# One-hots that read their row of numbers from a PSUM bank instead of SBUF, in a fused graph, attention and expert kernel

## What is computed

```python
def sage(x, src, dst, Wl, bl, Wr):
    agg = segment_sum(x[src], dst, N_NODES)          # gather the source rows, add them per destination
    cnt = segment_sum(ones, dst, N_NODES)
    return (agg / maximum(cnt, 1.0)[:, None]) @ Wl.T + bl + x @ Wr.T

h   = relu(sage(xn, src, dst, W1l, b1, W1r))          # layer 1
gnn = sage(h, src, dst, W2l, b2, W2r)                 # layer 2
mix = layer_norm(mlp(x1) + x1),  x1 = layer_norm(linear_attention(xn) + xn)
x   = x + gnn + mix
x   = x + prob * (gelu(ln(x) @ W1 + b1) @ Wd[expert] + bd[expert])   # the best of 8 experts for each node
```

## Time and profile before

| | us |
|---|---|
| three executions | 2453.99, 2454.78, 2458.47 |
| median | 2454.78 |
| the profiled execution, its own time | 2453.61 |
| its span in the trace | 2451.8 |
| PE busy | 1925.4 (79%) |
| POOL busy | 1702.3 (69%) |
| DVE busy | 1148.8 (47%) |
| ACT busy | 549.0 (22%) |

### The profile page before, as it was taken

How to read it: one execution, slowest core, us unless ns; L and a number is a source line. 1 busy time by engine, 2 the same in 40 slices (tenths; PEclk the granted TensorE clock), 3 DMA queues, 4 the chain that set the end, 5 groups by cost and what they waited for, 6 DMA issues and landing times.

```text
span 2451.8 us, 45561 instructions
## 1 busy us (share of the span) xinstructions
PE 1925.4 (79%) x9589; PEld 1190.2 (49%) x9590; DVE 1148.8 (47%) x3201; ACT 549.0 (22%) x1242; POOL 1702.3 (69%) x1773
## 2 busy tenths in 40 slices
PE   3799988878688887776899999877665543679998
PEld 2455555544455555543455555444332211368886
DVE  8544443433577777764555545433332221242221
ACT  6444333333222222221222222111100000101110
POOL 6777777777777777757777777777777777164442
PEclk9999999898899999997899999988776665689999
DMA  7444444444444444434454555444443333245551
GB/s 219 132 124 126 124 123 121 122 118 118 132 135 137 133 133 137 132 97 149 146 166 151 164 157 164 147 153 142 138 141 116 114 116 105 89 141 167 168 167 63
DMA packets 155000, 332.67 MB, mean 136 GB/s; under 512 B 34853, under 2 KB 89095, under 8 KB 154917
## 3 DMA queue, kind: packets, MB, share of 16 engines
q0 software_dynamic: 85824, 248.21, 34.6%
q10 hardware_dynamic: 42630, 58.35, 6.9%
q1 hardware_dynamic: 26466, 25.33, 3.4%
HBM read 273.97 MB, written 58.72 MB: 136 GB/s over the span
## 4 chain that ended last, share of the span: by engine, by line
PE 36%; POOL 33%; issue 15%; DVE 7%; DMA 4%; DVEq 2%; POOLq 2%; ACT 1%; ACTq 1%; SPq 0%
POOL big L699 32%; PE bank L538 12%; PE bank L1728 8%; PE bank L1496 6%; PE bank L1716 2%; PE bank L1502 2%; DMA mbuf<-qT_d 1%; PE bank L1526 1%; PE bank L1651 1%; PE bank L1521 1%; DMA big<-hh_d,edges 1%; POOL big L709 1%; POOLq L696 1%; DMA big<-xh_d,edges 1%; POOLq L694 1%
## 5 line engine op out<-in xcount | busy, mean ns | idle before, releaser
L699 POOL DMA_INDIRECT big<-xh_d,edges x782 | 769.8, 984 | 240.5 <-issue 232.4
L699 POOL DMA_INDIRECT big<-hh_d,edges x782 | 752.4, 962 | 261.1 <-issue 227.2
L1496 PE MATMUL bank<-big,S 128*128 x1960 | 589.0, 427 | 245.8 <-SPq L604 218.4
L898 DVE SCALAR_TENSOR_TENSOR S<-edges,tv,iota 128x512 f16<-128x512 f16 x490 | 368.6, 754 | 450.5 <-PE bank L1496 267.6
L1496 PEld LDWEIGHTS bank<-big,S 128*128 128x128 f16 x1960 | 203.7, 104 | 533.6 <-issue 389.8
L1494 PE MATMUL bank<-ones,S 128*128 128x1 f16 x980 | 165.4, 169 | 73.7 <-SPq L604 63.6
L538 PE MATMUL bank<-turned,x1T 128*128 128x512 f32 x392 | 195.6, 622 | 0.0
L720 POOL DMA_INDIRECT out_dram<-big,node_s x56 | 56.8, 1014 | 145.1 <-DVE big L1231 141.2
L1494 PEld LDWEIGHTS bank<-ones,S 128*128 128x128 f16 x980 | 95.5, 97 | 89.5 <-SPq L604 75.7
L1424 ACT ACTIVATE x1T<-bank 128x256 f32<-128x256 f32 x49 | 18.8, 383 | 531.7 <-PE bank L1502 531.7
L1231 DVE SCALAR_TENSOR_TENSOR big<-bank,prob_s,res 128x256 f32<-128x256 f32 x56 | 27.1, 484 | 179.4 <-PE bank L1730 179.4
(11 more groups left out here) (228 smaller groups left out, 2910.4 us busy)
## 6 DMA issues: line engine op xcount, KB each, us to landing
hx_d<-mbuf ACTq DMA_DIRECT2D x49, 512.0 KB
big<-xh_d,edges POOLq DMA_INDIRECT x782
big<-hh_d,edges POOLq DMA_INDIRECT x782
big<-in_fwd_dram SPq DMA_DIRECT2D x8, 1024.0 KB, 6.4
qT_d<-abuf ACTq DMA_DIRECT2D x49, 128.0 KB
hh_d<-HL ACTq DMA_DIRECT2D x49, 128.0 KB
mbuf<-qT_d ACTq DMA_DIRECT2D x49, 128.0 KB, 2.6
hx_d<-res ACTq DMA_DIRECT2D x49, 128.0 KB
```

What stands on the lines that cost most here:

```text
L699: e.indirect_dma_start(G[:, r, n % SC, :], None, table, bass.IndirectOffsetOnAxis(ap=srcx[:, n:n + 1], axis=0)).then_inc(d_g[r], 16)
L898: VI.done(e.scalar_tensor_tensor(S[:, walk.u, :, :], dst[:, bass.ds(c * SC, SC)].unsqueeze(2).to_broadcast([P, SC, P]), tv[:, bass.ds(k, 1 ...
L1496: ins = e.matmul(AGG[:], S[:, walk.u, j, :], G[:, bass.ds(slot, 1), j, :].rearrange("p a c -> p (a c)"), start=False, stop=False, skip_gro ...
```

## The change

`numbers_p` is a quarter of the bank `FO`, which now belongs to DVE alone: DVE writes the numbers 0 to 127 there once, in fp32, and every one-hot reads them from there. `iota16` is gone. Another part of the same bank (`m_p`) takes the place of `m_t` in the attention's steps `tz`, `s`, `n2` and `res` (`m_t` stays for layer 2's normalised rows). To free `FO`, layer 1's product goes to the second half of `B5` (`FU`), beside the queries, and layer 2's product to the second half of `FT` (`FV`), beside the turned mean. As two engines are not to be in one bank at once, PE gets two waits: in layer 1, behind `tr1` of tile t, for the ReLU of tile t-1; in layer 2, ahead of `tr1` of tile t, for `x2` of tile t-1.

```diff
-        iota16 = sb("iota16", [P, P], F16)
...
+        FU, FV = B5[:, C:2 * C], FT[:, C:2 * C]
+
+        numbers_p, m_p = FO[:, 0:P], FO[:, C:2 * C]
...
-            step(e.tensor_copy(iota16[:], ii[:, 0:P]))
             step(e.tensor_copy(iof[:, 0:P + 3], ii[:]))
...
+            step(e.tensor_copy(numbers_p, iof[:, 0:P]))
...
                 VI.done(e.scalar_tensor_tensor(
                     S[:, walk.u, :, :], dst[:, bass.ds(c * SC, SC)].unsqueeze(2).to_broadcast([P, SC, P]),
-                    tv[:, bass.ds(k, 1)], iota16[:].unsqueeze(1).to_broadcast([P, SC, P]),
+                    tv[:, bass.ds(k, 1)], numbers_p.unsqueeze(1).to_broadcast([P, SC, P]),
                     ALU.subtract, ALU.is_equal), "S")
...
                 step("tz", at(lambda: e.tensor_tensor(
-                    m_t.rearrange("p (h q m) -> p h q m", h=CH, m=HD), blocks[:, :, 0:P].rearrange("p h (q m) -> p h q m", m=HD),
+                    m_p.rearrange("p (h q m) -> p h q m", h=CH, m=HD), blocks[:, :, 0:P].rearrange("p h (q m) -> p h q m", m=HD),
...
-                step("s", at(lambda: e.scalar_tensor_tensor(m_s[:], xnS, rstd[:, bass.ds(raw(i), 1)], m_t[:], ALU.mult, ALU.add)))
+                step("s", at(lambda: e.scalar_tensor_tensor(m_s[:], xnS, rstd[:, bass.ds(raw(i), 1)], m_p, ALU.mult, ALU.add)))
...
-                step("n2", mo(lambda: e.scalar_tensor_tensor(m_t[:], m_o, lnt[:, 2:3], lng2, ALU.subtract, ALU.mult)))
+                step("n2", mo(lambda: e.scalar_tensor_tensor(m_p, m_o, lnt[:, 2:3], lng2, ALU.subtract, ALU.mult)))
...
-                step("res", mo(lambda: e.scalar_tensor_tensor(res_tile(i - 2), m_t[:], lnt[:, 7:8], res_tile(i - 2),
+                step("res", mo(lambda: e.scalar_tensor_tensor(res_tile(i - 2), m_p, lnt[:, 7:8], res_tile(i - 2),
                                                               ALU.mult, ALU.add)))
...
-                    VX2.done(e.tensor_tensor(res_tile(t), res_tile(t), FO[:, 0:C], ALU.add), "x2")
+                    VX2.done(e.tensor_tensor(res_tile(t), res_tile(t), FV, ALU.add), "x2")
...
-                    AR1.done(e.activation(hb[:], FO[:, 0:C], ACT.Relu), "relu")
+                    AR1.done(e.activation(hb[:], FU, ACT.Relu), "relu")
...
                     clear(AGG[:])
                     clear(CNT[:, 0:1])
                     PT1.done(transposes(FT, 0, mean), "tr1")
+                    AR1.wait(e, "relu", t, 1)
...
                     clear(AGG[:])
+                    VX2.wait(e, "x2", t, 1)
                     PT2.done(transposes(FT, 0, mean), "tr1")
```

More of the change, by code:

```diff
@@ L1520, in out1 @@
                     for h in range(CH):
-                        e.matmul(FO[:, 0:C], xTs[:, h, :], w1r[:, h, :], start=(h == 0), stop=False)
-                    e.matmul(FO[:, 0:C], ones3[:], gb1, start=False, stop=False)
+                        e.matmul(FU, xTs[:, h, :], w1r[:, h, :], start=(h == 0), stop=False)
+                    e.matmul(FU, ones3[:], gb1, start=False, stop=False)
                     if isinstance(t, int):
@@ L1525, in out1 @@
                     for h in range(CH):
-                        ins = e.matmul(FO[:, 0:C], mT[:, h, :], w1l[:, h, :], start=False, stop=(h == CH - 1))
+                        ins = e.matmul(FU, mT[:, h, :], w1l[:, h, :], start=False, stop=(h == CH - 1))
                     PH1.done(ins, "h")
@@ L1628, in out2 @@
                     AM2.wait(e, "mT", t)
-                    PO2.done(matmuls(e, FO[:, 0:C], [(mT[:, h, :], w2l[:, h, :]) for h in range(CH)]), "o")
+                    PO2.done(matmuls(e, FV, [(mT[:, h, :], w2l[:, h, :]) for h in range(CH)]), "o")
                 def trx(t):
```

## The result

The changed kernel takes 2435.86 us (median of 4; 2432.62 to 2436.64), the kernel before 2456.62 us beside it: ratio 0.991, 95% interval 0.9897 to 0.9924, so 20.8 us less. The profiled execution is the longest of its four, 2436.64 us with a span of 2434.8, against the shortest of before (2453.61): between the two profiles lie 17.0 us. Every ratio in this document is taken over the executions in the faster of a chip's two states alone, and so can differ a little from the quotient of the medians beside it.

A forecast was written before the change was run, and what follows sets the result against it. POOL's gathers, at a beat of about 1.25 us, were taken to set the pace except where PE or DVE steps do. Savings of 12.3 + 6.4 + 0.7 + 5.0 = 24.4 us gave 2430 us, range 2424 to 2438.

The forecast's parts named there:

- the first gather of layer 2 would start 19 us earlier: Sign at the start of layer 2: its first gather comes some 19 us earlier if the forecast holds.
- One-hots stop holding gathers.: All 490 one-hots: they no longer lengthen gathers; in the stretch 75 to 635, 12.3 us saved and kept.
- The term of 19.4 us for layer 1: Layer 1: 12.3 us from 75 to 635, plus stage B's 6.4 from one-hots and 0.7 from step `s`.
- It is kept, with 1.5 us to spare: Stage B: its saving of 6.4 and 0.7 us is kept, POOL's least room of 4.4 us exceeding the 2.9 needed.
- the 4.8 us are lost: Layer 2 up to 1362: the 4.8 us of shorter gathers are lost, as POOL waits longer for PE.
- Layer 2 behind 1362: 5.0 us.: Layer 2 behind 1362: 5.0 us saved and kept, since POOL's room grows again.
- A PSUM operand costs nothing.: DVE steps using the bank: price taken as 0, bounded by 63 ns each; the one-hot stays at 754 ns.
- PE's wait for the ReLU is covered.: Layer 1: PE's new wait costs 0; at stage B's tightest tile the ReLU ends 0.78 us before `tr1`.
- dearer operands: Rival, DVE steps with PSUM operands: 63 ns more each, still faster than before, 2436 us; chance 0.14.
- half rate: Rival, one-hots: numbers stream from PSUM at half rate, 0.53 us more each, slower at 2457 to 2458 us; chance 0.05.
- More is kept: Rival: layer 2's early saving isn't lost, or gathers meet remaining two-input steps less often; 29.2 us saved, 2425 us; chance 0.06.
- Doesn't unlock: Rival: something else in the one-hot holds gathers (index operand, fp16 output, length); 2454 us, up to 2460; chance 0.07.

The follow-up runs named there:

- after_again: The changed kernel as it is, compared a second time with the kernel before: 2435.47 us against 2457.55, ratio 0.9909.
- numbers_in_sbuf_again: The changed kernel with the one-hots reading the numbers from SBUF in fp32, on a faster chip: 2461.31 us against 2460.12 for the kernel before, ratio 1.0002.
- waits_only: The kernel before with only TensorE's two new waits added: 2459.43 us against 2457.66, ratio 1.0005.
- psum_layer2_only_again: The changed kernel with layer 1's one-hots reading from SBUF, layer 2's from the bank, on a faster chip: 2455.56 us, ratio 0.9991 to the kernel before.
- psum_layer1_only_again: The changed kernel with layer 2's one-hots reading from SBUF, layer 1's from the bank, on a faster chip: 2440.57 us, ratio 0.9923 to the kernel before.
- numbers_in_sbuf: The changed kernel with the one-hots reading the numbers from SBUF in fp32, on the slower chip: 3169.42 us against 3134.63 for the kernel before, ratio 1.0143.
- psum_layer1_only: The changed kernel with layer 2's one-hots reading from SBUF, layer 1's from the bank, on the slower chip: 3159.92 us, ratio 1.0084 to the kernel before.
- psum_layer2_only: The changed kernel with layer 1's one-hots reading from SBUF, layer 2's from the bank, on the slower chip: 3192.2 us, ratio 1.0149 to the kernel before.
- psum_layer2_early: The changed kernel with only the one-hots of layer 2's first 15 turns reading from the bank, on the slower chip: 3163.33 us, ratio 1.0117.

## Why the prediction was right, and where its terms were off

Forecast: 24.4 us less, 2430 us, range 2424 to 2438. Measured: 20.8 us less, 2435.9 us. The forecast named as signs that the first gather of layer 2 would start 19 us earlier and the last one end near 2072. They came 15.1 us earlier and at 2080.8 in the first profile, and 22.3 us earlier and at 2073.5 in `after_again`. So the mechanism and the main terms were right, while the agreement of the sum is helped by the spread between executions, which is as large as what is missing.

1. *One-hots stop holding gathers.* Right: 141 long gathers blamed on them became none, the mean of the first stretch came out at the forecast 958 ns, and with the operand back in SBUF the gain is gone (1.0002).
2. *The term of 19.4 us for layer 1* is 18.5 in the profiled execution and 21.4 in `after_again` (1007.7 to 989.2 and 986.3); layer 1 alone gave 17 to 19 us of the whole. The size was right.
3. *"It is kept, with 1.5 us to spare"*, of stage B, is the step that failed, and the prediction had named it itself as a sign of being wrong: "if POOL waits for PE in stage B". POOL did wait, at the very superchunk of the earlier trace rows and nowhere else in stage B, 3.2 us in one profile and 0.5 in the other. The saving was worked out rightly: just ahead of that place POOL's gathers had come 15.3 us closer to the first one, against 12.3 + 2.9 = 15.2. The room was not. It took for granted that stage B comes 12.3 us earlier as a whole. But its first step `s` came 11.9 and 12.8 us earlier in the two executions, and the sum that frees the slot only 7.8 (825.61 to 817.79) and about 11.3. The first 46 turns of stage B, counted from one `s` to the next, took 411.8 us before and 417.1 and 412.2 in the changed kernel. In other kernels they took 411.5, 413.2 and 415.0 with layer 1's one-hots in SBUF (`numbers_in_sbuf_again`, `waits_only`, `psum_layer2_only_again`), and 417.5 with them in the bank (`psum_layer1_only_again`). So the length of stage B differs by more than the 1.5 us between executions, and whether the change itself makes it longer is not shown. One thing that lengthens it can be seen. In 637 to 988 us, the second of the small steps that follow a norm's statistics, before and after:

```profile
L435 DVE TENSOR_SCALAR lnt<-lnt 128x2 int32<-128x2 int32 x38 | 6.6, 173 | 1.3
...
L437 DVE TENSOR_SCALAR lnt<-lnt 128x2 int32<-128x2 int32 x38 | 7.8, 206 | 1.3
L1051 DVE TENSOR_SCALAR mbuf<-m_s,lnt 128x256 f32<-128x256 f32 x38 | 16.7, 439 | 1.4
```

   This is the lock seen from the other side: up to 1100 us, 12 of these steps of the changed kernel took more than 0.2 us, and 9 of them ended 4 to 9 ns before the end of a running gather; before, one step did, and ended so too. L1049, now L1051, took 418 ns there before (its mean over the kernel is 421). Why they met gathers more often was not tried.
4. *The handover between the layers* had no term. It took 17.9 us before, 21.1 in the first profile and 16.7 in the second. Before, the last `s` of stage B started 1.8 us ahead of the end of the last gather of layer 1; in the changed kernel it started 6.1 and 3.0 us behind it. So DVE still has stage B's last steps to do when the last gather has been issued, and the uncertainty of the item above comes in here too.
5. *Layer 2 up to 1362: "the 4.8 us are lost".* Right in kind: the waits for PE grew from 5.4 to 15.6 us. But the stretch also got longer, 260.6 to 265.2 us, and it took 263.9 to 268.8 in five more executions with the products moved, save for the one with shorter norms (258.4); the 268.8 are of `psum_layer1_only_again`, whose profiled execution is the slowest of its five (2447.79 us). It was 263.3 and 262.2 in two more with the products where they were. So the two executions of the changed kernel lost 1 to 5 us there, of the 5 that the late stretch gave, where the prediction had put no loss; the ranges with and without the moved products (263.9 to 268.8, 260.6 to 263.3) nearly touch. The waits are not the cause (`waits_only`), nor is the one-hots' operand (`numbers_in_sbuf_again` has 265.0). Nor is it PE's clock: over the first 100 us of layer 2 the granted clock was 0.78 before and 0.79 and 0.78 in the changed kernel. Moved products, branches, or chance are left; this stays open.
6. *Layer 2 behind 1362: 5.0 us.* It took 735.1 us before and 729.6 after: 5.5. Right in size.
7. *A PSUM operand costs nothing.* Right: the one-hot takes 747 ns, and step `s` 481 against 485. The two steps that write to PSUM take 432 (`tz`) and 484 ns (`n2`) in stage B, 6 to 7 more than the 425 and 478 before. The Trainium skill ("Perfetto Trace Analysis", section "Optimizing Scalar/DVE Operations") gives figures by which an estimate would be 65 ns more for an operand in PSUM; the one-hot shows none of it.
8. *PE's wait for the ReLU is covered.* Right: the smallest cover in stage B is 0.91 us in the first profile of the changed kernel and 0.84 in the second, and the two waits alone measure 1.0005.

The Trainium skill ("SBUF — State Buffer", section "Who interferes with whom") states that a DVE instruction with two SBUF inputs contends with a GpSimd instruction that reads SBUF; `numbers_in_sbuf_again` agrees. Its inference that descriptor generation is not touched by such an instruction does not hold for these gathers, 84 and 62 of which were held by one-hots in that run.

Of the rivals, "dearer operands" and "half rate" are out by the 747 ns. "More is kept" is out as it was put: layer 2's early saving is lost, since the stretch did not get shorter in the changed kernel. "Doesn't unlock" is out by `numbers_in_sbuf_again`.

## What to carry to other kernels

Where an engine issues gathers at a fixed beat and sets the pace, look for instructions of another engine that end just where a long gather ends, and for one form that never does; the difference between the forms tells which operand to move. Count the saving only in the stretches where that engine sets the pace, and don't trust a margin smaller than the spread of the stretch between executions. And a kernel with such a lock can get slower when a turn gets shorter, most likely since the number of meetings depends on the turn's length against the beat; this is worth knowing before a good edit is thrown away.

## What was not expected of the hardware

The first four runs (`numbers_in_sbuf`, `psum_layer1_only`, `psum_layer2_only`, `psum_layer2_early`) were on a chip where the kernel before takes 3134.63 us (29 executions, 3101 to 3163) instead of 2456, at a mean granted clock of 0.80 instead of 0.89. Of `numbers_in_sbuf` there, the chain by engine, and the longest wait of POOL:

```profile
PE 32%; issue 23%; another core or an unknown queue 15%; DVEq 13%; DVE 9%; ACT 3%; ACTq 3%; POOL 1%; DMA 1%; SPq 0%; POOLq 0%
```

```profile
POOL big L701 <- PE bank L1498: 635.8, 133, 13.7
```

The instructions of POOL and DVE are as long as elsewhere (gathers 978 and 965 ns, one-hots 753), and PE is busy for 2123 us instead of 1920. Most of the 700 us lie between the instructions: from 100 to 500 us, a quarter of the chain (25.6%) waits for something that the profile calls another core or an unknown queue. POOL waits 636 us for PE and is 1% of the chain. With POOL no longer the pace, the holds can matter little, and what costs nothing elsewhere has a price: with the moved products, waits and bank steps alone the kernel is 1.4% slower than before, and 0.8% with layer 1's one-hots in the bank, though those two intervals overlap. Which of the three costs the time was not tried. The full change was not run there, so its effect on that chip is open, as is what makes the chip slow.
